# A fused attention and MLP kernel on one core: stages two and three in pieces of four or two tiles, another split of the PSUM banks, another order of loads

## The reference

```python
def _prob(x):
    x = jnp.tanh(x) * 0.499 + 0.5
    return jnp.clip(x / (jnp.sum(x, axis=-1, keepdims=True) + EPS), EPS)
# q = layernorm(x) without gain; k = v = ctx
q_prob, k_prob = _prob(q), _prob(k)
log_ratio = jnp.log(q_prob) - jnp.log(k_prob)
sid = jnp.einsum('bnd,bmd->bnm', q_prob - k_prob, log_ratio)
attn = jax.nn.softmax(-sid / D ** 0.5, axis=-1)
attn_feat = jnp.einsum('bnm,bmd->bnd', attn, v)
f_diff = (v - attn_feat) @ W_diff.T + b_diff + q
h = _layernorm(f_diff, ln_g, ln_b)
mlp = jax.nn.gelu(h @ W1.T + b1, approximate=False) @ W2.T + b2
x = x + _layernorm(mlp + f_diff, ln_g, ln_b)
# then x = x + ffn(layernorm(x)): inputs and weight rounded to float8 e4m3,
# one 128 x 128 product, plus a bias
```

## Time and profile before

| what | value |
|---|---|
| median of 3 runs | 270.52 us (270.42 to 270.64) |
| profiled execution, its own time | 270.51 us |
| its span in the profile | 268.5 us |
| mean granted TensorE clock | 0.93 of full speed |
| busy over the span | PE 210.2, DVE 220.8, ACT 203.4, POOL 156.2 us |
| the same as shares | PE 78%, DVE 82%, ACT 76%, POOL 58% |
| stages, from the timeline | one to 67 us, two to 130 us, three and its drain to the end |
| chain that ended last, by engine | PE 46%, DVE 23%, ACT 19%, DMA 4%, issue 4%, POOL 2% |

### The profile page before, as it was taken

How to read it: one execution, slowest core, us unless ns; L and a number is a source line. 1 busy time by engine, 2 the same in 40 slices (tenths; PEclk the granted TensorE clock), 3 DMA queues, 4 the chain that set the end, 5 groups by cost and what they waited for, 6 DMA issues and landing times.

```text
span 268.5 us, 5871 instructions
## 1 busy us (share of the span) xinstructions
PE 210.2 (78%) x1767; PEld 179.0 (67%) x1767; DVE 220.8 (82%) x860; ACT 203.4 (76%) x731; POOL 156.2 (58%) x203
## 2 busy tenths in 40 slices
PE   2557666653698888885799999999999999999230
PEld 1456654433586666664699998999999898998120
DVE  1888999989969999999525788889988888879961
ACT  4499999998579999997856666677778666676520
POOL 2375777776666555573353577666666677755550
PEclk9999799995579999999999999999999999999755
DMA  5875555520000000000094347577888777774677
GB/s 152 231 146 163 164 153 168 154 76 1 1 0 2 2 0 5 2 0 2 0 103 57 35 47 78 75 97 104 122 118 119 105 100 105 94 95 73 119 109 148
DMA packets 44767, 22.33 MB, mean 83 GB/s; under 512 B 2240, under 2 KB 44608, under 8 KB 44736
## 3 DMA queue, kind: packets, MB, share of 16 engines
q0 software_dynamic: 16896, 8.39, 27.5%
q1 hardware_dynamic: 27408, 13.38, 19.3%
q10 hardware_dynamic: 432, 0.20, 0.3%
HBM read 9.37 MB, written 4.19 MB: 51 GB/s over the span
## 4 chain that ended last, share of the span: by engine, by line
PE 46%; DVE 23%; ACT 19%; DMA 4%; issue 4%; POOL 2%; SPq 0%; DVEq 0%; POOLq 0%; ACTq 0%
PE bank L884 21%; ACT TQK L415 6%; ACT TQK L431 6%; DVE q_c L663 6%; DVE F L686 6%; DVE LN_c L671 6%; PE bank L874 5%; PE bank L875 5%; PE bank L876 5%; DMA LN_c<-in_ctx_dram 3%; ACT PV L426 3%; PE bank L904 2%; ACT vT_c L420 2%; DMA F<-rows 2%; PE bank L829 1%
## 5 line engine op out<-in xcount | busy, mean ns | idle before, releaser
L884 PE MATMUL bank<-W2T,TQK 128*128 128x128 f32 x512 | 68.1, 279 | 0.0
L884 PEld LDWEIGHTS bank<-W2T,TQK 128*128 128x128 f32 x512 | 64.5, 191 | 4.1
L507 ACT ACTIVATE TQK<-bank,b1c 128x512 f32<-128x512 f32 x64 | 43.9, 687 | 24.4 <-PE bank L876 24.3
L336 POOL TENSOR_SCALAR q_c<-TQK,GAINK,SHIFT 128x128 f32<-128x128 f32 x64 | 32.1, 518 | 20.5 <-PE bank L849 19.9
L874 PE MATMUL bank<-hTh,W1h 128*128 128x512 f32 x64 | 29.2, 456 | 1.6 <-DVE hTl L759 1.6
L318 POOL TENSOR_TENSOR xrstd<-xvar,pow_c 128x4 f32<-128x4 f32 x16 | 16.8, 1052 | 23.0 <-DVE xvar L591 23.0
L377 POOL TENSOR_TENSOR ovar<-sso,eps_c 128x4 f32<-128x4 f32 x16 | 3.1, 192 | 44.5 <-ACT TQK L521 44.5
L875 PE MATMUL bank<-hTl,W1h 128*128 128x512 f32 x64 | 25.4, 396 | 0.0
L876 PE MATMUL bank<-hTh,W1l 128*128 128x512 f32 x64 | 25.2, 394 | 0.0
L783 PE MATMUL bank<-ident,LN_c 128*128 128x128 f32 x64 | 11.7, 312 | 17.1 <-DMA LN_c<-in_ctx_dram 17.1
L705 DVE TENSOR_TENSOR F<-bank,F 128x512 f32<-128x512 f32 x16 | 11.1, 691 | 16.9 <-PE bank L884 13.3
(11 more groups left out here) (119 smaller groups left out, 624.3 us busy)
## 6 DMA issues: line engine op xcount, KB each, us to landing
F<-rows POOLq DMA_DIRECT2D x32, 256.0 KB, 5.1
LN_c<-in_ctx_dram SPq DMA_DIRECT2D x16, 256.0 KB, 3.0
X<-in_x_dram SPq DMA_DIRECT2D x16, 256.0 KB, 3.4
out_dram<-F SPq DMA_DIRECT2D x16, 256.0 KB, 4.3
LN_c<-in_L_xattn_W_dram SPq DMA_DIRECT2D x1, 256.0 KB, 6.5
lT_c<-in_L_xattn_W_dram SPq DMA_DIRECT2D x1, 256.0 KB, 5.4
...
```

Source lines behind the costliest of these rows:

```text
L336: last = pool.tensor_scalar(tile(diff_c, k, i), all_tile(TK, k, i), per_tile(GAINK, k, i, 1), per_tile(SHIFT, k, i, 1), ALU.mult, ALU.add)
L507: act.activation(buf(hid_c, m, HB * C)[:, j * C:(j + 1) * C], M1_B[j % 2][:, :], ACT.Gelu, bias=b1c[:, j:j + 1]).then_inc(gelu_ready, 1)
L884: last = pe.matmul(M2_B[m.buf][:, i * D:(i + 1) * D], buf(hid_c, m, HB * C)[:, j * C + i * D:j * C + (i + 1) * D], W2T[:, j * D:(j + 1) * ...
```

## The change

Stage one keeps its 16 chunks (now called `chunks`). Stages two and three run over `pieces`: 14 of four tiles and then four of two tiles, 18 in all (NP). Further:

- SP loads x and ctx of five chunks first, then W1, chunk 5, W2, chunk 6, the small vectors, the other chunks, and last the three rows. PE's work on W1 and W2 moves from step 2 to step 7 (`W_AT` = 6), two of the three copies behind it from ACT to DVE, the third to ACT's step 10.
- EP has one pair of banks, 5 and 6 (for a piece of two tiles one bank of them), and waits for `f_ready` of the piece before. `M1_B` is banks 1, 2 and 7, and the two banks of the MLP's output are 3 and 4. mlp1(j) now waits for the gelu of three blocks back instead of two.
- PE turns h of piece 0 in stage two's step 18 and runs its first two mlp1 blocks in step 19, ahead of that step's EP; ACT's first two gelus of it stand in its step 20 of stage two. take_h(0) is in DVE's step 17, the lower half in step 18.
- For the last two pieces DVE adds the bias bf instead of the DMA. In steps that take no more h, DVE finishes the moments before the quantised copy.

The diff, cut to its core:

```diff
+    chunks = pieces_of([G] * NC)
+    pieces = pieces_of([G] * (NC - 2) + [2] * 4)
+    NP = len(pieces)
...
-        D_B, L_B, S_B, EP_B = bank[2], bank[3], (bank[4], bank[7]), ((bank[5], bank[6]), (bank[0], bank[1]))
-        M1_B, M2_B, HT_B, XQ_B, FF_B = (bank[0], bank[1]), (bank[2], bank[3]), bank[4], bank[5], bank[6]
+        D_B, L_B, S_B, EP_B = bank[2], bank[3], (bank[4], bank[7]), (bank[5], bank[6])
+        M1_B, M2_B, HT_B, XQ_B, FF_B = (bank[1], bank[2], bank[7]), (bank[3], bank[4]), bank[0], bank[5], bank[6]
+        def m1_bank(k, j):
+            return M1_B[(HB * k.n + j) % 3][:, 0:k.g * D]
+        def ep_bank(k, i):
+            return EP_B[i // 2 if k.g == G else k.buf]
...
+        W_AT = 6
+        BF_HERE = NP - 2
...
-            for n in range(2):
-                load(Chunk(0, n, 0, NC))
+            for k in chunks[0:5]:
+                load(k)
             sp.dma_start(W1_raw.rearrange("p (j d) -> p j d", d=D),
                          W1.rearrange("(j p) d -> p j d", p=P)).then_inc(w_in, 16)
+            load(chunks[5])
             sp.dma_start(W2_raw, W2).then_inc(w_in, 16)
+            load(chunks[6])
...
# ACT, stage one
-                if is_chunk(k, 0):
-                    act.wait_ge(w_ps, 1)
+                if is_piece(k, W_AT + 2):
+                    act.wait_ge(w1u_sb, 1)
                     act.wait_ge(w_in, 16 * 5)
-                    act.activation(W1u, bank[3][:, :], ACT.Copy)
-                    act.activation(W1h[:, :], bank[3][:, :], ACT.Identity, scale=g_col[:, 0:1])
-                    act.activation(W2T[:, :], bank[4][:, :], ACT.Copy).then_inc(w_sb, 1)
+                    act.activation(W1h[:, :], W1u, ACT.Identity, scale=g_col[:, 0:1]).then_inc(w_sb, 1)
# DVE, stage one
+                if is_piece(r, W_AT):
+                    dve.wait_ge(w_ps, 1)
+                    dve.tensor_copy(W1u, bank[3][:, :]).then_inc(w1u_sb, 1)
+                if is_piece(r, W_AT + 1):
+                    dve.tensor_copy(W2T[:, :], bank[4][:, :]).then_inc(wt_sb, 1)
...
# DVE, stage two
-                if is_chunk(k, NC - 2):
+                if is_piece(k, NP - 3):
                     dve.wait_ge(frstd, 1)
-                    take_h(Chunk(0, 0, 0, NC))
+                    take_h(pieces[0])
+                if is_piece(k, NP - 2):
+                    lower_half(pieces[0])
...
# DVE, stage three, quantise(q)
+                if q.n >= BF_HERE:
+                    dve.wait_ge(xq_ready, q.n + 1)
+                    dve.tensor_tensor(tiles(chunk(F, q)), tiles(chunk(F, q)), over_tiles(bf_r, q.g),
+                                      ALU.add).then_inc(bf_done, 1)
...
# PE, stage two
                 k = at(2)
+                if is_piece(k, NP - 2):
+                    turn_h(pieces[0])
+                if is_piece(k, NP - 1):
+                    mlp1(pieces[0], 0)
+                    mlp1(pieces[0], 1)
                 if k.live:
                     pe.wait_ge(e_ready, k.n + 1)
-                    wait(pe, f_ready, k.n - 1)
+                    wait(pe, f_ready, k.n)
```

More of the change, by code:

```diff
@@ L20, with __init__, pieces_of, is_piece @@
 E4M3_SAFE = 128.0
[L23 to L30 removed]
+class Piece:
+    def __init__(self, n, at, g):
+        self.n, self.at, self.g, self.buf, self.live = n, at, g, n % 2, True
+NO_PIECE = Piece(-1, 0, 0)
+NO_PIECE.live = False
+def pieces_of(sizes):
+    return [Piece(n, sum(sizes[:n]), g) for n, g in enumerate(sizes)]
 def wait(eng, sem, count):
[L35 removed]
+    if count <= 0:
         return
     eng.wait_ge(sem, count)
[L40 to L48 removed]
+def is_piece(k, n):
+    return k.live and k.n == n
+def run_steps(pieces, last_lag, step):
+    for n in range(len(pieces) + last_lag):
+        step(lambda lag, n=n: pieces[n - lag] if 0 <= n - lag < len(pieces) else NO_PIECE)
 def xattn_ffn_kernel(nc, x, ctx_in, W_diff, b_diff, ln_g, ln_b, W1, b1, W2, b2, Wf, bf, out):
@@ L291, in store @@
                 wait(sp, y_ready, k.n + 1)
[L292 to L296 removed]
+                sp.dma_start(out_d[:, k.at:k.at + k.g], tiles(chunk(F, k))).then_inc(stored, 16)
+            for k in pieces:
+                store(k)
+            sp.wait_ge(stored, 16 * NP)
         @block.gpsimd
```

503 lines of the change are left out of this document (253 added, 250 removed).

## The result

The changed kernel took 269.18 us in the median of 20 runs (267.2 to 271.24), the one before 270.55 on the same chip; the ratio is 0.9938, 95% [0.9914, 0.9962], so 1.7 us faster where 3.9 were forecast. The 20 runs form two groups, ten from 267.2 to 268.6 and ten from 269.8 to 271.2, and the median lies in the gap between them. The profiled execution is one of its longer ones: 270.56 us for a span of 268.7, the same as before's 270.51 for 268.5. Its mean granted clock is 0.918, the page's PE has 218.1 us busy, 7.9 more.

A forecast was written before the change was run, and what follows sets the result against it. Stage one was taken as bound by ACT, two by DVE and ACT, three by PE, then a drain. From 270.5 us: loads -2.9, one pair 0, handover +0.7, stage three 0, tail -1.7 gave 266.6, range 263.6 to 269.3.

The forecast's parts named there:

- the tail: Last pieces: DVE becomes the bound, PE waits for lower halves, the bias DMA wait goes; -1.7 us, from +0.8 to -4.
- the 0 of stage three: Stage three: PE's work and 7.5 us pitch stay until the small pieces arrive, so 0.
- The handover, +0.7: Stage two to three: first MLP blocks 1.4 us earlier, but EP(17), F(17), take_h(1) follow them; +0.7 us, from -2.3 to +2.0.
- the prediction's chain: Handover: from F(15) at about 125.7 us, steps one after another through take_h(1) and its turn to the second-layer product at 132.8.
- The rival of the lower clock: Stage two: TensorE at half clock, each such period costs 2.3 us; three additional ones make 273.5 us; chance 0.08.
- The loads, -2.9: Stage one: second ctx chunk 2.0 us earlier and copies moved off ACT save 2.9 us, from 0.9 to 4.8.
- that rival: Stage one: DVE takes ACT's place as bound, only 0.9 us is gained, total 268.6 us; chance 0.15.
- One pair, 0: Stage two: EP waits for F and slips some 0.2 us, ACT and POOL still find the turns; 0 at full clock.
- A fixed cost per piece: Rival, handover and tail: half-size operations cost three quarters, handover some 1.5 us worse, tail's gain halved, total 269.0; chance 0.10.

The follow-up runs named there:

- the filled version: The changed kernel with transposes that nothing reads put into TensorE's idle time in late stage two and the handover: 268.12 us, ratio 0.9892 to the kernel before.

## Why the prediction was wrong

Its number was 2.6 us too low: 269.18 against 266.6, at the upper edge of its range of 263.6 to 269.3. The direction was right. Of its terms the tail and the 0 of stage three (-0.31) held.

- **The handover, +0.7, is the step that failed.** The order of events was foreseen: blocks early, then EP(17), F(17), take_h(1), the turn, and the product no earlier. At full clock the handover is 1.05 to 1.7 us longer than before (18.26, 18.66 and 18.94 against 17.21), inside the bounds and above the term: from the end of F(15) to the product the prediction's chain has 7.1 us, and it took 7.7. What the prediction left out is the clock: it priced the blocks, EP and turns by rows at full clock. In all three profiles it halved there, the same way took up to 10.0, and the term is +2.9 to +3.65. The rival of the lower clock had the mechanism and put it in the wrong stretch: stage two's periods kept 1.00. The rows of before didn't settle it, since PE did nearly the same in both kernels ahead of the place. The same stretch, of the changed kernel and of the one before:

```profile
122.00:126.00 4.00, 2.47 (x26) 1.72 (x25) 3.41 (x11) 3.80 (x16) 3.46 (x8) 0.97 0.02 4
```

```profile
122.00:126.00 4.00, 2.63 (x40) 1.92 (x37) 3.45 (x13) 2.37 (x10) 1.18 (x3) 1.00 0.01 4
```

PE was busy 2.47 of 4 us, then its clock fell; 2.63 of 4, and it did not. Nor was there a long pause: in the 12 us ahead of the fall PE was never idle for more than 0.99, 1.23 and 0.98 us at a time in the three profiles. What makes it fall in one execution and not in another stays open. The lower level belonged into the upper bound. In the median of many runs the fall weighs less than in the profiled execution: the filled version is 1.2 us faster by the two ratios, and their intervals overlap.

- **The loads, -2.9, were mis-sized:** -1.95 in this profile, -2.1 in the mean. The ctx chunk came at 8.04 instead of 7.5, PE was late once more (0.23), and the W1h copy took 0.61 of ACT as expected. DVE didn't become the bound; that rival fell.
- **One pair, 0, was mis-sized.** The prediction saw the turns slip by 0.2 us and had ACT and POOL "still find them". They do, but the slip puts POOL's start where DVE's q_c group takes 1.21 instead of 1.09. That is where the +0.94 until F(11) comes from; against the mean of the eleven profiles with two pairs, which can be as slow (3.58), it is 0.5. At the end the tie costs 0.7 us more.
- The Trainium skill, GPSIMD Engine Reference, section 1, says that POOL shares its SBUF interfaces with VectorE, with contention for DVE instructions with two SBUF inputs. The prediction weighed this for Wf alone. The traces agree here too: the q_c group, with two inputs from SBUF, takes 1.05 without POOL and up to 1.28 beside it, while F's group, which reads a bank, takes 1.05 beside POOL (89.25 to 90.30).
- **The tail, -1.7, measured -1.62, and its mechanism is in the trace:** DVE is the bound and takes 30.77 us from output(13) on, 30.9 in the prediction's count. What it did not see is that the small pieces earn none of it. With the bias on DVE and chunks of four the drain is 131.0, with small pieces 131.4 to 131.8. The whole gain is the removed wait for the DMA (2.4 alone); the rest of the change gives 0.4 to 0.8 of it back, and the shorter last store returns 0.5. It is not the pieces that give it back: with full ones and the rest of the change the drain is 131.90. The other order of DVE's steps and the other banks were not separated.
- *A fixed cost per piece* explains little: ACT's copy of 256 columns took 0.27 to the next row where one of 512 took 0.48, a share of 0.56 and not three quarters. The prediction said that no row of before shows an operation of half size on ACT, but there is one in every period, the exponential, with 0.26:

```profile
91.59 0.41 ACT L466 ACTIVATE E_c<-bank 128x256 f32<-128x256 f32 x1
91.85 0.63 ACT L474 ACTIVATE vT_c<-bank 128x512 f32<-128x512 f32 x1
```

So of the change two edits carry 4.9 us (loads and bias), and the rest (small pieces, one pair, the blocks ahead of EP(17)) costs 3.2 of them: 0.9938 - 0.9819 = 1.2%. The blocks' place alone is 2.6 of it, the clock's share included.
